# Attention's first stage reordered: keys by token half into eight banks, key and value weights split on DVE, low gathers on ScalarE

## What is computed

```
def _layernorm(x, axis=-1, eps=1e-05):
    m = jnp.mean(x, axis=axis, keepdims=True)
    v = jnp.var(x, axis=axis, keepdims=True)
    return (x - m) / jnp.sqrt(v + eps)
...
q = (x @ wq.T).reshape(b, t, N_HEADS, HEAD_DIM).transpose(0, 2, 1, 3)
k = (x @ wk.T).reshape(b, t, N_KV_HEADS, HEAD_DIM).transpose(0, 2, 1, 3)
v = (x @ wv.T).reshape(b, t, N_KV_HEADS, HEAD_DIM).transpose(0, 2, 1, 3)
k_full = jnp.repeat(k, group, axis=1)
v_full = jnp.repeat(v, group, axis=1)
scores = jnp.einsum('bhtd,bhsd->bhts', q, k_full) / np.sqrt(HEAD_DIM)
mask = _sink_window_mask(t)[None, None, :, :]
attn = _masked_softmax(scores.astype(jnp.float32), mask).astype(x.dtype)
out = jnp.einsum('bhts,bhsd->bhtd', attn, v_full)
out = out.transpose(0, 2, 1, 3).reshape(b, t, N_HEADS * HEAD_DIM)
return out @ wo.T
...
x = x + _L0_attn_a_ref(_layernorm(x, axis=-1), wq, wk, wv, wo)
```

## Time and profile before

| | us |
|---|---|
| median of 3 runs | 574.26 |
| lowest, highest | 574.2, 577.9 |
| the profiled execution's own time | 574.69 |
| its span, first to last instruction | 572.9 |
| PE busy | 523.3 (91%) |
| DVE busy | 410.5 (72%) |
| ACT busy | 304.3 (53%) |
| POOL busy | 131.5 (23%) |

### The profile page before, as it was taken

How to read it: one execution, slowest core, us unless ns; L and a number is a source line. 1 busy time by engine, 2 the same in 40 slices (tenths; PEclk the granted TensorE clock), 3 DMA queues, 4 the chain that set the end, 5 groups by cost and what they waited for, 6 DMA issues and landing times.

```text
span 572.9 us, 9040 instructions
## 1 busy us (share of the span) xinstructions
PE 523.3 (91%) x3031; PEld 439.2 (77%) x3033; DVE 410.5 (72%) x894; ACT 304.3 (53%) x752; POOL 131.5 (23%) x274
## 2 busy tenths in 40 slices
PE   1798899999999979889999999999999889999994
PEld 1577699999999967677887887757778668788884
DVE  6734366666666878889968797966886768886674
ACT  3435677787688643363433454888662245343251
POOL 5511152534342320000000003669443000000000
PEclk9999999999999999999999999999999999999998
DMA  7310010000002103000030000000000000000101
GB/s 269 108 66 1 2 38 0 2 1 2 2 2 72 73 1 133 2 1 0 1 128 2 1 1 1 1 2 1 1 1 2 0 1 1 1 2 0 38 0 38
DMA packets 5790, 14.25 MB, mean 25 GB/s; under 512 B 624, under 2 KB 2928, under 8 KB 5744
## 3 DMA queue, kind: packets, MB, share of 16 engines
q1 hardware_dynamic: 5744, 13.66, 6.8%
HBM read 12.61 MB, written 1.05 MB: 24 GB/s over the span
## 4 chain that ended last, share of the span: by engine, by line
PE 66%; DVE 19%; ACT 6%; issue 6%; POOL 1%; DMA 1%; DVEq 0%; SPq 0%; ACTq 0%; POOLq 0%
PE psum L167 55%; PE psum L446 3%; DVE f_t L1170 2%; DVE f_um L1180 2%; DVE xn L227 2%; PE psum L477 1%; DVE ln_stats L207 1%; DVE oT_hl L665 1%; DMA x_resid<-in_x 1%; PE psum L964 1%; DVE x_resid L672 1%; ACT f_sil L1077 1%; DVE xT_hl L249 1%; ACT qT L540 1%; PE psum L1578 1%
## 5 line engine op out<-in xcount | busy, mean ns | idle before, releaser
L167 PE MATMUL psum<-xT_hl,ffn_w_hl 128*128 128x512 f32 x312 | 78.2, 397 | 7.3 <-DVE f_t L1170 7.3
L167 PE MATMUL psum<-f_um,ffn_w_hl 128*128 128x512 f32 x288 | 72.0, 398 | 1.2 <-DVE f_um L1180 1.2
L167 PEld LDWEIGHTS psum<-xT_hl,ffn_w_hl 128*128 128x128 f32 x312 | 56.3, 188 | 19.6 <-issue 8.7
L167 PEld LDWEIGHTS psum<-f_um,ffn_w_hl 128*128 128x128 f32 x288 | 53.5, 188 | 14.2 <-DVE f_um L1180 2.1
L1170 DVE TENSOR_TENSOR f_t<-psum,f_sil 128x512 f32<-128x512 f32 (+1 forms) x48 | 33.1, 690 | 32.8 <-ACT f_sil L1077 32.2
L1077 ACT ACTIVATE f_sil<-psum 128x512 f32<-128x512 f32 (+1 forms) x48 | 28.2, 595 | 51.9 <-PE psum L167 51.9
L167 PE MATMUL psum<-wo_hl,oT_hl 128*128 128x256 f32 x384 | 50.9, 282 | 4.0 <-DVE oT_hl L665 3.9
L659 DVE TENSOR_TENSOR pT_hl<-psum,pT_hl 126x360 fp32r<-126x360 f32 (+1 forms) x44 | 23.6, 537 | 42.9 <-ACT pT_hl L572 42.9
L167 PE MATMUL psum<-xT_hl,wq_hl 128*128 128x512 f32 x192 | 52.2, 407 | 1.9 <-ACT qT L540 1.9
L167 PEld LDWEIGHTS psum<-wo_hl,oT_hl 128*128 128x128 f32 x384 | 47.7, 188 | 7.5 <-DVE oT_hl L665 5.9
L1098 ACT ACTIVATE f_ch_hl<-f_ch 128x512 fp32r<-128x512 f32 x48 | 30.0, 630 | 41.3 <-DVE f_ch L1227 41.2
(11 more groups left out here) (238 smaller groups left out, 1129.1 us busy)
## 6 DMA issues: line engine op xcount, KB each, us to landing
w_raw<-in_wq SPq DMA_DIRECT2D x4, 512.0 KB, 3.2
w_raw<-in_wo SPq DMA_DIRECT2D x4, 512.0 KB, 3.3
ffn_w_raw<-in_ffn SPq DMA_DIRECT2D x3, 576.0 KB, 6.1
ffn_w_raw_far<-in_ffn SPq DMA_DIRECT2D x3, 576.0 KB, 6.5
ssd_w_raw<-in_ssd SPq DMA_DIRECT2D x3, 512.0 KB, 5.5
x_resid<-in_x SPq DMA_DIRECT2D x2, 512.0 KB, 4.6
out_x<-x_resid SPq DMA_DIRECT2D x4, 256.0 KB, 2.3
w_raw<-in_wk SPq DMA_DIRECT2D x1, 512.0 KB, 6.7
```

Of the source, the lines that this page charges most:

```text
L167: i = e.matmul(dst, lhs(a), rhs(b), start=start and n == 0, stop=stop and n == len(TERMS) - 1, **kw)
```

## The change

DVE normalises the first token half before it takes the statistics of the second. ACT writes the high part of the first half ahead of the weights' high parts. The low parts of wk (in two pieces of two heads each, `wk_lo`) and of wv are made on DVE, not on POOL, and POOL waits for them before it starts on the block of wq0. PE multiplies the keys of all heads for the first token half, into banks 4 to 7, then those of the second, into banks 0 to 3, with the transposes of the second half placed behind three heads' worth of keys of the first. The copies out of PSUM go by head and half. Both parts of `xg_hl` are now written by ACT. PE gets eight added matmuls of 128x256 in plain 32-bit type (`keep_busy`), whose result in bank 7 nobody reads: two before the first transposes, six between them and the keys.

```
--- before.py
+++ after.py
@@ -285,7 +285,7 @@
             NEGM, DEN, DENG, RDEN = (small[:, 192 + 16 * i:208 + 16 * i].rearrange("p (b h) -> p b h", b=4) for i in range(4))
 
             s_raw = [sem(f"w_raw{n}") for n in range(4)]
-            s_wh, s_wl = sem("att_w_hi"), sem("att_w_lo")
+            s_wh, s_wl, s_wk = sem("att_w_hi"), sem("att_w_lo"), sem("att_wk_lo_first")
             s_pz, s_xg, s_kw = sem("probs_wide_zero"), sem("xg"), sem("k_window")
             s_k, s_kev, s_v, s_vhi, s_vlo = sem("k_mm"), sem("k_ev"), sem("v_mm"), sem("v_hi"), sem("v_lo")
             s_q, s_qt, s_mask = sem("q_mm"), sem("q_ev"), sem("masked")
@@ -375,6 +375,14 @@
                 e.wait_ge(s_wh, n + 1)
                 e.tensor_tensor(part(n, LO), raw[:, n % 4, :], f32(part(n, HI)), ALU.subtract).then_inc(s_wl, 1)
 
+            def wk_lo(e, pair):
+
+                e.wait_ge(s_wh, 1)
+                seg = slice(pair * 2 * HD, (pair + 1) * 2 * HD)
+                wk_raw = raw[:, 0, :].rearrange("p (k n) -> p k n", k=KB)
+                e.tensor_tensor(wk_hl[:, LO, :, seg], wk_raw[:, :, seg], f32(wk_hl[:, HI, :, seg]),
+                                ALU.subtract).then_inc(s_wl if pair else s_wk, 1)
+
             windowed = [u for u, (g, j) in enumerate(units) if j]
 
             def out_view(ap, j):
@@ -396,22 +404,36 @@
                 return copy(xg_hl[:, which, k, :, 0:SINK], f32(repeat(xT[:, which, k, 0:SINK], NJ - 1)))
 
             def pe(e):
+                def keep_busy(n):
+
+                    for _ in range(n):
+                        e.matmul(bank(7)[:, 0:2 * P], ident, cf[:, 0:2 * P], start=True, stop=True)
+
+                def keys(g, h):
+                    if h == 0:
+                        if g in (0, 2):
+                            e.wait_ge(s_wk if g == 0 else s_wl, 1)
+                    for k in range(KB):
+                        m = three(e, bank(4 * (1 - h) + g), lambda w: wk_hl[:, w, k, g * HD:(g + 1) * HD],
+                                  lambda w: xT[:, w, k, HALF * h:HALF * h + HALF], k == 0, k == KB - 1)
+                    m.then_inc(s_k, 1)
+
                 e.wait_ge(s_cf, 16)
-                for h in range(2):
-                    ln["tr"](e, h)
+                keep_busy(2)
+                ln["tr"](e, 0)
+                keep_busy(2)
+                e.wait_ge(LN["hi"], 1)
+                keep_busy(2)
+                e.wait_ge(LN["hi"], 2)
+                keep_busy(2)
                 ln["ready"](e, 0)
+                for g in range(KV - 1):
+                    keys(g, 0)
+                ln["tr"](e, 1)
+                keys(KV - 1, 0)
+                ln["ready"](e, 1)
                 for g in range(KV):
-                    if g == 0:
-                        e.wait_ge(s_wl, 1)
-                    if g >= 2:
-                        e.wait_ge(s_kev, g - 1)
-                    for h in range(2):
-                        if g == 0 and h == 1:
-                            ln["ready"](e, 1)
-                        for k in range(KB):
-                            m = three(e, bank(2 * (g % 2) + h), lambda w: wk_hl[:, w, k, g * HD:(g + 1) * HD],
-                                      lambda w: xT[:, w, k, HALF * h:HALF * h + HALF], k == 0, k == KB - 1)
-                    m.then_inc(s_k, 1)
+                    keys(g, 1)
 
                 def queries(n):
                     g, h = n // (2 * GROUP), n % GROUP
@@ -430,7 +452,7 @@
                 def scores(u):
                     g, j = units[u]
                     if u == 0:
-                        e.wait_ge(s_kev, KV)
+                        e.wait_ge(s_kev, 2 * KV)
                     if u >= 2:
                         e.wait_ge(s_mask, u - 1)
                     e.wait_ge(s_qt, g * 2 * GROUP + (GROUP if Q0[j] + QN[j] <= HALF else 2 * GROUP))
@@ -452,6 +474,7 @@
                         scores(FIRST_UNITS[j])
                     if j == 0:
                         e.wait_ge(s_wl, 2)
+                        e.wait_ge(s_kev, KV)
                     if j == 1:
                         e.wait_ge(s_xg, 2 * KB)
                     if j >= 2:
@@ -521,14 +544,17 @@
                 early(phase, "base_x0", e)
 
             def act(e):
+                ln["hi"](e, 0)
                 w_hi(e, 0)
                 w_hi(e, 1)
                 w_hi(e, 2)
-                for h in range(2):
-                    ln["hi"](e, h)
+                ln["hi"](e, 1)
+                e.wait_ge(LN["hi"], 2 * KB)
+                for k in range(KB):
+                    gather(e, lambda o, i: e.activation(o, i, ACT.Copy), HI, k).then_inc(s_xg, 1)
                 ln["ready"](e)
                 for k in range(KB):
-                    gather(e, lambda o, i: e.activation(o, i, ACT.Copy), HI, k).then_inc(s_xg, 1)
+                    gather(e, lambda o, i: e.activation(o, i, ACT.Copy), LO, k).then_inc(s_xg, 1)
 
                 def q_evac(n):
                     h, half, g = n % GROUP, n // GROUP % 2, n // (2 * GROUP)
@@ -595,21 +621,27 @@
                         early(phase, "hi0", e)
 
             def dve(e):
-                for h in range(2):
-                    ln["stats"](e, *range(HT * h, HT * h + HT))
-                    ln["veps"](e, h)
-                for h in range(2):
-                    ln["norm"](e, h)
-                for h in range(2):
-                    ln["lo"](e, h)
-                ln["ready"](e)
-                for k in range(KB):
-                    gather(e, e.tensor_copy, LO, k).then_inc(s_xg, 1)
+                def keys_out(g, h):
+                    e.wait_ge(s_k, KV * h + g + 1)
+                    e.tensor_copy(kT[:, g, HALF * h:HALF * h + HALF], bank(4 * (1 - h) + g)).then_inc(s_kev, 1)
+
+                ln["stats"](e, *range(HT))
+                ln["veps"](e, 0)
+                ln["norm"](e, 0)
+                ln["stats"](e, *range(HT, NT))
+                ln["veps"](e, 1)
+                ln["lo"](e, 0)
+                wk_lo(e, 0)
+                wk_lo(e, 1)
+                ln["norm"](e, 1)
+                keys_out(0, 0)
+                ln["lo"](e, 1)
+                keys_out(1, 0)
+                w_lo(e, 1)
+                for g in range(2, KV):
+                    keys_out(g, 0)
                 for g in range(KV):
-                    e.wait_ge(s_k, g + 1)
-                    b0 = 2 * (g % 2)
-                    keys = PS[:, b0:b0 + 2, :].rearrange("p b n -> p (b n)")
-                    e.tensor_copy(kT[:, g, :], keys).then_inc(s_kev, 1)
+                    keys_out(g, 1)
 
                 def recip(u):
                     rows, parts, p = probs(u)
@@ -692,7 +724,7 @@
             def pool(e):
                 def gather_keys(w):
                     g, j = units[windowed[w]]
-                    e.wait_ge(s_kev, g + 1)
+                    e.wait_ge(s_kev, KV + g + 1)
                     if w >= W_SLOTS:
                         e.wait_ge(s_s, windowed[w - W_SLOTS] + 1)
                     k0 = kT[:, g, Q0[j] - WINDOW:T]
@@ -718,7 +750,8 @@
                 e.memset(pz[:, :, :, :], 0.0).then_inc(s_pz, 1)
                 ln["rstd"](e, 0)
                 ln["rstd"](e, 1)
-                for n in range(5):
+                e.wait_ge(s_wl, 2)
+                for n in range(2, 5):
                     w_lo(e, n)
                 e.wait_ge(s_pz, 1)
                 gathered = 0
```

## The result

The changed kernel took 568.32 us in the median of four runs (568.16 to 568.36), beside 575.9 for four runs of the kernel before (574.2 to 577.9). The ratio is 0.9861, 95% interval 0.9833 to 0.9889: faster by 1.1 to 1.7%. I had said 568.8 us, a gain of 5.5, and put 0.45 on more than 1% and 0.52 on no more than that; the measured ratio lies beyond 1%. The profiled executions are 574.69 and 568.28 us long, their spans 572.9 and 566.5: 6.4 us between like and like.

A forecast was written before the change was run, and what follows sets the result against it. The chain of waits holding PE back before its first long run was taken as the bound. Keys at 14.6 plus 12.85 put the values at 27.45 against 32.90, 5.5 us earlier: 568.8 us, range 567.0 to 571.3.

The forecast's parts named there:

- `xn` and POOL: First stage: DVE's long `xn` wait for POOL's `w_lo` to finish, which costs 6 us.
- The rival of the weights' loads: First stage: weight loads, not POOL, stretch the `xn`; gain about 3 us, 571 us; chance 0.03.
- The sum from the keys' start to the values: First stage on PE: 4.2 + 0.95 + 1.96 + 5.6 + 0.1 = 12.85 us from first key to first value product.
- The keys' start: First key matmul on PE, behind the six `keep_busy`: at 14.6 us, between bounds of 12.9 and 15.2.
- early clock: PE's clock rises so soon that keys start between 12.9 and 14.0; gain 6.1 to 7.1 us; chance 0.33.
- the three estimates I had made for their end: End of the six `keep_busy` before the keys, for three moments of the clock's rise: 14.1, 14.9 or 15.1 us.
- The rule I weighed: Transposes don't count for PE's clock: rise near 15.0 us, sum about half a microsecond smaller.
- called it covered: ACT's low gathers, 2.8 us, end before the first value product needs ACT's work, by 0.3 us only.
- The gain is kept: Later stages hang on this chain by semaphores alone, so the 5.5 us reach the end.

The follow-up runs named there:

- experiment 1: The kernel before, with POOL's five weight splits made to wait for all eight `xn`; lowest 574.57 us, ratio 1.0026 to the kernel before.
- experiment 4: The changed kernel with the low parts of wk and wv back on POOL; lowest 569.07 us, ratio 0.9898 to the kernel before.
- experiment 9: The changed kernel with the second half's transposes behind one head's keys instead of three, second time; lowest 568.01 us, ratio 0.9875 to the kernel before.
- experiment 2: The kernel before, with POOL's splits waiting for the `xn` and the low gathers on ACT; lowest 568.23 us, ratio 0.9906 to the kernel before.
- experiment 3: The changed kernel with the low gathers back on DVE, behind wv's low part; lowest 576.43 us, ratio 1.0028 to the kernel before.
- experiment 12: The kernel before, with POOL's wait, low gathers on ACT and four `keep_busy`; lowest 568.13 us, ratio 0.9895 to the kernel before.
- experiment 8: The changed kernel with the second half's transposes behind one head's keys instead of three, first time; lowest 567.22 us, ratio 0.9888 to the kernel before.

## Why the prediction was right

**`xn` and POOL.** Right, and shown by experiments 1 and 4 from both sides. The rival of the weights' loads is dead.

**The sum from the keys' start to the values.** 12.85 us forecast, 12.79 measured, and each term within 0.1 us: 4.20 for 18 keys, 0.89 for the transposes, 2.00 to the second half's keys, 5.70 to the values. ACT kept more room than I had given it (0.3 us forecast, 0.78 left).

**The keys' start.** This term was mis-sized: 14.6 forecast, 13.28 measured. 0.3 us of it is an earlier start of the six `keep_busy` (9.60 for 9.9), most of it a load of x that landed 0.2 earlier; the rest is the clock, which rose at about 11.8 us, 4.2 after the first transposes, so that the six took 3.7 us rather than 4.7. That is the rival "early clock" (keys between 12.9 and 14.0). It isn't fixed: in experiment 9 an execution took 4.91 us for the same six products. Of the three estimates I had made for their end (14.1, 14.9, 15.1) only the first lies inside what executions then did (12.8 to 14.4). The rule I weighed (the Trainium skill, "TensorE: Matmul & The Clock Gate", Part 4, that transposes don't count as PE activity) fails here: in experiments 1 and 2 the only PE work before the keys was 16 transposes in 3.3 us, and then the first 24 keys of experiment 1 took 5.83 us, 0.243 each, the 2.4 GHz level from the start. So stretched `xn` had cost the kernel before twice, in waiting and in twelve slow keys behind broken-up transposes.

**The total.** On the profiled pair it was 1.32 us more for the keys' start and 0.06 more for the sum, against 0.4 lost behind the values: 5.5 forecast, 6.4 measured, inside the rival's 6.1 to 7.1. That the median came within 0.5 us of 568.8 is partly luck. I had counted from 574.26, the median of three runs; from the 575.9 beside the result the same gain would have given 570.4.

**What the low gathers are for.** I saw only the cost of their move to ACT and called it covered. The profile before couldn't show what it prevents, since there the gathers ran at 20.8 to 22.7 us while POOL was idle (17.5 to 24.6). Experiments 1 and 3 show that without their move the gain is lost. It didn't spoil the sum only because the change moved both, which is luck as far as my reasoning goes.

**The later stages.** "The gain is kept" holds for the profiled pair but for 0.4 us. The medians moved by more, 7.6 us in the first session, most likely through falls of the clock, which I hadn't counted and which no part of the change explains.

## What to carry to other kernels

When one engine's instructions all end with another engine's, suspect a shared path, and before moving the other's work look at what it will run beside next: the collision may return ten microseconds later with a longer queue behind it. Test a big change by its smallest subset; here two edits came within 0.2 us of its lowest time. Where the spread of runs exceeds the effect, compare the distance between two landmarks in the traces: a single landmark moved by 1.5 us between executions of the same code. And don't trust four tight runs.

## What the runs showed of the hardware

A DVE copy between SBUF tiles waits for the POOL subtraction beside it, however small it is: 40 elements took 0.18 us alone and 2.42 beside POOL; 1098 elements, 0.79 alone, took 2.99 in experiment 1 and ended 0.65 us after POOL's. I had written that DVE waits for POOL and not the reverse. In two places it was the reverse: POOL's subtraction, 2.42 us as a rule, took 2.86 in experiment 1 and 2.77 in experiment 3 where such a copy of DVE was already under way. Copies out of PSUM didn't suffer: in the changed kernel four copies of 512 keys took 2.48 us beside POOL's split at 22.1 us, 0.62 each. ACT's six gathers of the same tiles took 2.78 us beside it, as without.

TensorE's clock rose after transposes alone: the 16 of experiments 1 and 2 took 3.27 and 3.33 us, 3.68 in experiment 12 where the clock was still low behind them, and the keys after them ran at the 2.4 GHz level. The moment of the rise moved by some 3 us between executions of the same code (experiments 8 and 9: 1.6 us more for six products that take twice as long at the low level).
